# Folding each batch's eight products to four on GpSimd ahead of VectorE's sum, in a one-core decoder layer

## The reference

```python
x = layernorm(x + attention(x))     # 16 query heads, 4 key heads of 128, rotary, softmax, output projection
x = layernorm(x + xattn(ctx, ctx, x))
x = layernorm(x + ffn(x))           # gate picks one of 16 heads, then attention over shared keys and values
```

```python
kv  = einsum('bhil,bhjl->bijhl', k, v)          # pair products of the context
out = causal_conv(kv, ssm_kernel) + kv * D
out = einsum('bijhl,bhil->bjhl', out, q)        # 8 products for each output channel, summed over i
```

## Time and profile before

| what | us |
|---|---|
| median of three runs (322.43 to 323.41) | 323.4 |
| the profiled execution, its own time | 322.93 |
| its span, first to last instruction | 321.1 |
| PE busy in the span | 305.8 |
| DVE, ACT, POOL busy in the span | 244.1, 231.1, 200.7 |

### The profile page before, as it was taken

The page is one execution under the profiler, slowest core; times in us unless marked ns, Lnnn a source line. Parts: engine busy times, 40 slices in busy tenths (PEclk is TensorE's granted clock), DMA queues, the critical chain, the costliest instruction groups (busy, mean ns, idle before and its releaser), DMA issues.

```text
span 321.1 us, 6269 instructions
## 1 busy us (share of the span) xinstructions
PE 305.8 (95%) x2073; PEld 241.7 (75%) x2073; DVE 244.1 (76%) x502; ACT 231.1 (72%) x693; POOL 200.7 (62%) x289
## 2 busy tenths in 40 slices
PE   6999899999999999999999999999999999999982
PEld 2788798889888888888888988877556666666650
DVE  2778968735876985775684998889989899987555
ACT  3699767868769867696686688634479777788890
POOL 0599766875573698477661278995987976721021
PEclk9999999999999999999999999999999999999996
DMA  6950212020010311404000000000000000000001
GB/s 188 328 238 1 65 36 98 3 90 9 0 35 2 98 34 36 163 2 142 0 2 1 2 1 1 2 0 3 0 3 0 18 1 3 16 3 26 9 18 49
DMA packets 5760, 13.87 MB, mean 43 GB/s; under 512 B 864, under 2 KB 3040, under 8 KB 5472
## 3 DMA queue, kind: packets, MB, share of 16 engines
q1 hardware_dynamic: 5456, 13.08, 12.3%
q10 hardware_dynamic: 272, 0.39, 0.4%
HBM read 12.42 MB, written 1.05 MB: 42 GB/s over the span
## 4 chain that ended last, share of the span: by engine, by line
PE 74%; DVE 13%; ACT 4%; issue 4%; DMA 2%; POOL 1%; POOLq 0%; DVEq 0%; ACTq 0%
PE bank L402 18%; PE bank L549 11%; PE bank L439 7%; PE bank L424 7%; PE bank L660 4%; PE bank L671 4%; PE bank L510 4%; PE bank L618 3%; DVE t_cos L1781 3%; PE bank L683 2%; PE bank L655 2%; DMA w_raw<-in_wqkv 2%; PE bank L533 2%; PE bank L528 2%; PE bank L530 2%
## 5 line engine op out<-in xcount | busy, mean ns | idle before, releaser
L2288 POOL TENSOR_TENSOR t_sin<-rot,sin 128x512 f32<-128x512 f32 x36 | 46.8, 1308 | 32.8 <-ACT rot L1129 29.4
L2316 POOL TENSOR_TENSOR prob<-prob,rden 128x512 f32<-128x512 f32 x32 | 35.2, 1104 | 38.0 <-DVE rden L1681 38.0
L1164 ACT ACTIVATE prob<-bank,neg_max 128x128 f32<-128x128 f32 x128 | 45.6, 375 | 10.8 <-DVE neg_max L1674 9.5
L1244 ACT ACTIVATE prob<-bank,fneg_max 128x128 f32<-128x128 f32 x128 | 36.7, 379 | 6.3 <-DVE fneg_max L1838 6.3
L549 PE MATMUL bank<-wo_hi,head_hi 128*128 128x256 f32 x128 | 40.3, 314 | 0.5 <-DVE head_lo L1723 0.4
L549 PE MATMUL bank<-wo_hi,head_lo 128*128 128x256 f32 x128 | 36.0, 281 | 0.0
L549 PE MATMUL bank<-wo_lo,head_hi 128*128 128x256 f32 x128 | 36.0, 281 | 0.0
L1128 ACT COPY rot<-bank 64x512 f32<-64x512 f32 x40 | 23.4, 585 | 15.6 <-PE bank L402 14.6
L402 PE MATMUL bank<-x_hi,w_hi 128*128 128x512 f32 x96 | 32.6, 421 | 1.7 <-DVE w_hi L1642 1.7
L1595 DVE TENSOR_TENSOR t_cos<-bank,cos 128x512 f32<-128x512 f32 x36 | 24.6, 686 | 12.0 <-ACT rot L1129 11.3
L2278 POOL TENSOR_TENSOR kv<-ctxT 128x256 f32<-128x256 f32 (+3 forms) x64 | 33.1, 550 | 0.2 <-PE bank L424 0.2
(11 more groups left out here) (132 smaller groups left out, 800.9 us busy)
## 6 DMA issues: line engine op xcount, KB each, us to landing
w_raw<-in_wqkv SPq DMA_DIRECT2D x4, 768.0 KB, 4.4
toep<-in_toep SPq DMA_DIRECT2D x8, 256.0 KB, 3.0
wo_raw<-in_wo SPq DMA_DIRECT2D x4, 512.0 KB, 4.6
x_raw<-in_xt SPq DMA_DIRECT2D x2, 512.0 KB, 5.4
ctxT<-in_ctx SPq DMA_DIRECT2D x1, 1024.0 KB, 4.7
x<-in_x SPq DMA_DIRECT2D x1, 1024.0 KB, 8.9
out<-x SPq DMA_DIRECT2D x8, 128.0 KB, 1.7
wf<-in_wf SPq DMA_DIRECT2D x1, 784.0 KB, 4.4
```

The lines of the kernel that those rows point to most:

```text
L1164: last = act.activation(prob[:, k % 2, h * P:(h + 1) * P], score_bank[k % 2][:, h * P:(h + 1) * P], ACT.Exp, bias=neg_max[:, k % 2, h:h + ...
L1244: last = act.activation(prob[:, c % 2, h * P:(h + 1) * P], scored[:, h * P:(h + 1) * P], ACT.Exp, bias=fneg_max[:, c, h:h + 1])
L2288: pool.tensor_tensor(t_sin[:, par, :].rearrange("p (b t) -> p b t", b=BH), rot[:, par, :].rearrange("p (b t) -> p b t", b=BH), sin[:, :].u ...
L2316: pool.tensor_tensor(own, own, rden[:, k % 2, :].unsqueeze(2).to_broadcast([P, HG, P]), ALU.mult).then_inc(norm_done, 1)
```

## The change

`mix_sum` takes four in place of eight elements for each output (2048 to 1024 elements read, at a step: four of each eight). A new POOL instruction `fold(b)` adds the upper four onto the lower four, in place, 1024 elements, after it has waited on a new semaphore for POOL's own 15 products; `prod_done` is now counted by the fold. Beside it the lists of PE, ACT, DVE and POOL are changed in many places, in all stages, by moves of one to some places; no other instruction is added, removed or resized, and the transfers and their queue (SP) are untouched. The core of the diff, with the moves that lie around the second sublayer:

```diff
@@ DVE, mix_sum
-                dve.tensor_reduce(mixT[:, j, :], prod[j], axis=AX.X, op=ALU.add
+                dve.tensor_reduce(mixT[:, j, :], prod[j][:, :, :, 0:HD // 2], axis=AX.X, op=ALU.add
                                   ).then_inc(mixT_done, 1)
@@ POOL, products
                 last = pair_products(pool, b, j, distances)
                 if distances[-1] == HD - 1:
-                    last.then_inc(prod_done, 1)
+                    last.then_inc(terms_done, 1)
+
+            def fold(b):
+                terms = prod[b % 2].rearrange("p a j i -> p (a j) i")
+                pool.wait_ge(terms_done, b + 1)
+                pool.tensor_tensor(terms[:, :, 0:HD // 2], terms[:, :, 0:HD // 2], terms[:, :, HD // 2:HD],
+                                   ALU.add).then_inc(prod_done, 1)
@@ POOL, the list
             normalize(6, 2)
             sin_item(6, "Q2")
             sin_item(6, "Q3")
+            products(0, range(0, 3))
             normalize(6, 3)
-            products(0, range(0, 3))
             products(0, range(3, HD))
+            fold(0)
             normalize(7, 0)
             normalize(7, 1)
             products(1, range(0, 3))
+            normalize(7, 2)
             second_power(0)
-            normalize(7, 2)
             products(1, range(3, HD))
+            fold(1)
             normalize(7, 3)
             products(2, range(0, 4))
             second_power(1)
             products(2, range(4, HD))
+            fold(2)
             first_power(1)
             products(3, range(0, 4))
             second_power(2)
             products(3, range(4, HD))
+            fold(3)
             products(4, range(0, HD))
             add_ffn(0)
+            fold(4)
             second_power(3)
             third_power(0)
             products(5, NEAR)
             products(5, FAR)
+            fold(5)
             second_power(4)
             products(6, NEAR)
             products(6, FAR)
             add_ffn(1)
+            fold(6)
             second_power(5)
             third_power(1)
             products(7, NEAR)
             products(7, FAR)
+            fold(7)
             second_power(6)
+            second_power(7)
             add_ffn(2)
+            add_ffn(3)
             third_power(2)
-            add_ffn(3)
-            second_power(7)
...
@@ ACT, unit 6: mix_query(0) goes ahead of exps(6, 3)
-            head_copy(6, 0)
             item(6, "Q2")
             item(6, "Q3")
+            head_copy(6, 0)
+            mix_query(0)
             exps(6, 3)
             head_copy(6, 1)
             prob_high(6, 2)
-            mix_query(0)
...
@@ PE, around x2_turn(3), x2_turn(5) and x2_turn(6)
             fvalues(1, 1)
-            fturn(1, 2)
+            mix_turn(3)
             fscores(2, 0)
+            fturn(1, 3)
             x2_turn(3)
-            fturn(1, 3)
...
+            fturn(3, 2)
             x2_turn(5)
-            fvalues(3, 0)
+            fscores(4, 0)
             fvalues(3, 1)
...
-            fturn(4, 1)
+            fturn(4, 2)
             x2_turn(6)
             fscores(5, 0)
...
@@ DVE, around mix_sum(0) and around ffn_norm(0)
             invert(7, 0)
+            row_max(7, 2)
             invert(7, 1)
-            row_max(7, 2)
-            accumulate(6, 0)
+            mix_sum(0)
             head_low(6, 3)
-            mix_sum(0)
+            add_mix(0)
             prob_copy(7, 0)
...
+            first_apply(5)
+            first_apply(6)
+            ffn_norm(0)
+            add_mix(3)
             mix_norm(3)
-            ffn_norm(0)
+            frow_max(2, 0)
             second_apply(3)
...
```

More of the change, by code:

```diff
@@ L1335, in _ @@
             prob_high(2, 1)
-            split_wo(2)
+            exps(2, 3)
             head_copy(2, 1)
             item(2, "C10")
-            exps(2, 3)
             item(2, "C11")
@@ L2192, in _ @@
             mix_norm(4)
+            second_apply(4)
             y_invert(1)
-            frow_max(2, 3)
             y_scale(1)
-            second_apply(4)
             frow_max(3, 0)
+            frow_max(3, 1)
+            gating(4)
             mix_sum(5)
-            frow_max(3, 1)
-            add_mix(5)
-            gating(4)
-            mix_norm(5)
+            share(4)
             frow_max(3, 2)
             frow_max(3, 3)
-            share(4)
+            add_mix(5)
+            mix_norm(5)
+            y_invert(2)
+            ffn_norm(1)
             second_apply(5)
-            ffn_norm(1)
-            y_invert(2)
             mix_sum(6)
             frow_max(4, 0)
+            frow_max(4, 1)
             y_scale(2)
-            ffn_apply(1)
             add_mix(6)
-            frow_max(4, 1)
+            mix_norm(6)
             gating(5)
@@ L2217, in _ @@
             frow_max(4, 3)
-            mix_norm(6)
             share(5)
-            y_invert(3)
             second_apply(6)
             mix_sum(7)
+            ffn_apply(1)
+            y_invert(3)
             y_scale(3)
             frow_max(5, 0)
+            frow_max(5, 1)
             add_mix(7)
-            frow_max(5, 1)
-            ffn_norm(2)
-            mix_norm(7)
-            gating(6)
-            frow_max(5, 2)
-            frow_max(5, 3)
-            second_apply(7)
-            share(6)
+            mix_norm(7)
+            second_apply(7)
+            frow_max(5, 2)
+            gating(6)
+            frow_max(5, 3)
+            share(6)
+            ffn_norm(2)
+            ffn_apply(2)
             y_invert(4)
-            ffn_apply(2)
-            ffn_norm(3)
             y_scale(4)
@@ L2239, in _ @@
             frow_max(6, 1)
-            ffn_apply(3)
-            ffn_norm(4)
             gating(7)
             frow_max(6, 2)
+            share(7)
+            ffn_norm(3)
             frow_max(6, 3)
-            share(7)
             frow_max(7, 0)
```

600 lines of the change are left out of this document (300 added, 300 removed).

## The result

The changed kernel took 329.6 us, the median of six executions (327.1 to 337.1), the kernel before 323.4 (322.4 to 324.1). The ratio is **1.0158 [1.0128, 1.0188]**: 1.6% slower, 5.1 us. Slower was right; the forecast of 325.3 had 1.9 us of loss, and the time lies above the range (323.5 to 328). Executions more than 1.5% above the fastest of their kernel, which have a lower granted clock as well, are left out of every ratio here; for this kernel those are the two longest, 333.3 and 337.1 (clock 0.982 and 0.973, the others 0.989 to 0.998).

The account below looks back on a forecast made before the run. PE was taken to bound the kernel, with POOL becoming full in the second sublayer; the profiled 322.9 us plus a 2.2 us stall gave 325.1, put at 325.3 for the median (0.6% slower), range 323.5 to 328.

Parts of the forecast that it names:

- the prices: Second sublayer: a fold on POOL at 2.4 us, the halved `mix_sum` on DVE at 1.21 us, eight of each.
- the stall of 2.2 us at batch 3: PE at `x2_turn(3)`: 2.8 us later behind POOL's late `second_power(3)`, less 0.6 filled by a moved `fturn`.
- The list sum: POOL's instructions from 196.05 us to the end of `second_power(3)`, added up: 55.6 us, so ending at 251.7, before at 248.9.
- the prediction's own signs of being wrong: Fold under 2 us, batch 0's products starting before 194 us, or `second_power(3)` ending before 250 us.
- PE has one `fturn` moved ahead of it: PE's list before `x2_turn(3)`: a moved instruction of 0.6 us fills part of the 2.8 us delay.
- the loss made once: From batch 3 on, the loss holds at some 2 us; POOL's 11.1 us a batch is about PE's 11.4.
- the moves at nothing: Attention's reordered lists change no instruction and were taken at nothing, with 1 us either way.
- VectorE's gain at nothing: DVE saves 1.07 us a batch, 8.5 in all, but the halved sum is spent on waiting for the fold.
- 4.3 us on the chain: Four of eight `mix_sum` stand on the chain, worth at most this; PE could take back no more than 3.2 us.
- Rival 2: Faster, chance 0.18: folds at or under 1.85 us and early products let `mix_sum` give back 2.5 us, 320.9 us.
- contention at nothing: DVE and POOL sharing a port: at worst 1.3 us of waiting a batch, none of it counted in the forecast.
- rival 3: Slower still, chance 0.12: port waits of 1.3 us a batch on top of the stall, 2 us more, 327.5 us.

Follow-up runs that it names:

- half_no_fold: The changed kernel's orders without the fold, the sum over only the first four products, the upper four left out; 324.6 us, 1.0037 of the kernel before.
- fold_alone: The kernel before with its old orders, the fold put behind each batch's products and the sum over four; 335.5 us, 1.0376 of the kernel before.
- late_new: The kernel before with the changed kernel's orders only from the end of attention on, no fold, sums over eight; 1.0182 of the kernel before.
- half_old: The kernel before with only the sum cut to four of eight products, the upper four left out, no fold; 322.5 us, 0.9978 of the kernel before.
- three_waits: The changed kernel with three more GpSimd waits, at places where a VectorE instruction had been held 2 us or more; median 328.6 us, 1.0126 of the kernel before.
- power_first_wait: The changed kernel with second_power(3) to (6) each ahead of a fold, and fold(4) to (7) waiting for the previous batch's second_apply; 333.5 us, 1.0305 of the kernel before.

## Why the prediction was right or wrong

- **Right: the prices.** Fold 2.36 us (2.4), `mix_sum` 1.21 (1.21), POOL full: 87.2 of 91.7 us from 193.8 to 285.5.
- **Right in the power's time, wrong in cause: the stall of 2.2 us at batch 3, which was the whole forecast.** PE's wait at `x2_turn(3)` is 0.51 us. The list sum gave 251.7 for the end of `second_power(3)`, and it ended at 252.7 (252.14 and 0.55). But two errors lie in it, and they nearly cancelled, by luck. `products(0)` started at 193.86, not 196.05 (before 194, one of the prediction's own signs of being wrong); POOL then stood idle for VectorE's variances (0.86 and 0.96 us ahead of two powers). And the fold ahead of the power held it up by 0.2 us at most: without the fold the power starts at the same time. PE's list had put `mix_turn(3)` later, by 3.4 us even in half_no_fold, where `x2_turn(3)` stands at 252.34, 2.7 of its 3.6 us late without any fold. The step that failed is "PE has one `fturn` moved ahead of it": I looked at what moved between `x2_turn(3)` and its neighbour, and not at `mix_turn(3)`, which the power depends on. Nor was the loss made once: `x2_turn(5)` is 5.9 us late. In the old orders the power does wait for the fold, as fold_alone shows.
- **Wrong: the moves at nothing.** I gave the moves in attention 1 us either way and took the later ones as filling. Without the fold they cost 3.6 us together. The attention did end 2.2 us sooner at `x1_turn(0)` (190.92 against 193.10), and that lead is worth 2.3 us; the later moves cost 5.9 (late_new), and had eaten the lead by `mix_turn(0)` (207.28 against 207.48).
- **Wrong: VectorE's gain at nothing, and why.** 4.3 us on the chain, of which 3.2 for PE, was the bound. half_old shows 0.7, and PE's idle time in the stretch did not shrink there (3.3 to 3.7 us); in the new orders it is 2.4. The prediction had the gain spent on waiting for the fold; in the changed kernel VectorE is not idle ahead of any `mix_sum`. Rival 2's gain of 2.5 us is near the 2.4, but it was set against the old time, and the orders had cost 3.6 first.
- **Wrong: contention at nothing.** It was rival 3, at 0.12, and sized at 1.3 us a batch, spread evenly over five instructions. In the traces it is not even: most applies and key copies are held 0.6 us or less, and none to four in a profile take 1.6 to 3.8 us. The rows were there, but the price was cut to an average, and I let a hold end with one instruction. Rival 3's 327.5 is near the best executions (327.1), which is luck: it stands on the stall, and leaves out the orders and the halving.
- **Not foreseen: `normalize` behind the fold** in POOL's queue, 3.7 us of PE's waits in fold_alone and none in the changed kernel, where the moves hide it.

In the changed kernel, then, by its ratios: +3.6 from the orders, -2.4 from the halved sum, +3.9 from the fold, 5.1 in all. The 3.6 are 5.9 behind attention less 2.3 in it. Of the fold's part the runs show the held instructions (1.7 us at one key copy, 2.3 at one apply in one of two profiles; without them about half of the added idle time went, in three_waits) and, in power_first_wait, GpSimd's lateness; how it is divided in each execution they don't settle.

## What to carry to other kernels

An instruction's place on the chain is only a loose bound for what a shorter one gives (here 4.3 us): leave the work out without replacing it, and run that first; here it shows 0.7 us in the old orders and 2.4 in the new, less than the fold costs in either (12.9 and 3.9). Filling an idle engine that shares a way to memory with a busy one can hold up the busy one's short instructions, and what counts is whether PE waits behind the one that is held. A list that is reordered along with an edit is a change of its own: price what each moved step releases, not only what it passes.

## What the runs showed of the hardware

- **VectorE's hold can go on over many instructions of GpSimd**, not one of them: 3.49 us beside nine products of at most 0.56 us each, 3.77 beside four quarters and two others. It can also end at the first boundary, with no gap in the records: 0.97 us beside a fold in quarters, 0.73 beside products. What decides isn't shown. The Trainium skill ("SBUF — State Buffer", "Who interferes with whom") says that whoever issues first has the shared port pair for its whole instruction, and the other blocks; the rows agree that it blocks, and differ in the length, which here can go over instruction boundaries. That a reduction is not held agrees: `mix_sum` took 1.18 to 1.22 us, with GpSimd busy beside it.
- **A stop of PE can cost twice.** In fold_alone PE worked 0.55 of 2 us and then ran at half clock (PE's clock is the third column from the end):

```profile
220.00:222.00 2.00, 0.55 (x3) 0.55 (x4) 2.00 (x3) 0.00 (x0) 2.00 (x3) 0.88 0.01 4
222.00:224.00 2.00, 2.00 (x5) 1.02 (x4) 1.24 (x5) 0.88 (x3) 2.00 (x5) 0.50 0.00 0
224.00:226.00 2.00, 2.00 (x12) 1.69 (x10) 1.60 (x4) 0.38 (x1) 1.51 (x3) 0.77 0.00 0
```

  That is the level of 1.2 GHz. The wait of 1.84 us for the key copy in the changed kernel was followed by no fall, nor was that of 2.03 us at 206 to 208 in fold_alone itself.
